# The first layer's value bias and mask move to VectorE and GpSimd, and the second layer's preparation is cut into 28 steps

## What is computed

```python
# layer 0, 16 heads of 16 columns
xn = layer_norm(x, norm_w, norm_b)
q, k = xn @ q_w + q_b, xn @ k_w + k_b
att = softmax(q @ k.T + (1 - mask) * -1e6)          # per head, 256 x 256
v = (xn @ v_w + v_b) * src_mask[:, :, None]
y = att @ v
scale, shift = split(silu(emb) @ emb_w + emb_b)
x = x + silu(layer_norm(y) * (1 + scale) + shift) @ out_w + out_b
# layer 1: linear attention (softmax of q over the head's columns, of k over the rows),
# y = q @ (k.T @ v), then the same scale, shift, silu and product with film_out_W
```

## Time and profile before

| | |
|---|---|
| median of 3 runs | 976.47 us (976.24 to 977.93) |
| the profiled execution's own time | 977.76 us |
| its span | 976.0 us |
| mean granted TensorE clock | 0.982 |
| busy: PE | 916.1 us, 94% |
| busy: DVE | 772.6 us, 79% |
| busy: ACT | 709.6 us, 73% |
| busy: POOL | 581.9 us, 60% |

### The profile page before, as it was taken

One profiled execution on the slowest core, in us unless ns is written; L12 is line 12 of the kernel. 1 busy time (PEld: TensorE's weight loads), 2 busy tenths in 40 slices (PEclk: granted clock), 3 DMA queues, 4 the chain that ended last, 5 costly groups with the idle time before them and its releaser, 6 DMA issues.

```text
span 976.0 us, 24849 instructions
## 1 busy us (share of the span) xinstructions
PE 916.1 (94%) x8880; PEld 760.1 (78%) x8880; DVE 772.6 (79%) x1536; ACT 709.6 (73%) x1328; POOL 581.9 (60%) x1033
## 2 busy tenths in 40 slices
PE   5789999999999999999999767999999999999996
PEld 4666767777777777777776436999999999999995
DVE  5568988888888888888887733888888888888874
ACT  2257677777777777777777665788888888888874
POOL 3343636454545555555554224688888888888874
PEclk9999999999999999999999978999999999999998
DMA  8733333334343434343424112212233222223101
GB/s 263 242 113 116 136 137 136 138 123 150 115 158 118 154 115 159 112 156 115 158 103 147 67 60 86 68 45 77 77 91 99 78 76 77 77 86 97 43 29 54
DMA packets 77402, 108.62 MB, mean 111 GB/s; under 512 B 7072, under 2 KB 43392, under 8 KB 77152
## 3 DMA queue, kind: packets, MB, share of 16 engines
q1 hardware_dynamic: 77280, 107.03, 32.6%
HBM read 35.60 MB, written 16.88 MB: 54 GB/s over the span
## 4 chain that ended last, share of the span: by engine, by line
PE 82%; DVE 8%; issue 6%; POOL 2%; ACT 1%; SPq 0%; DMA 0%; POOLq 0%; DVEq 0%; ACTq 0%
PE psX L1041 14%; PE psY L1141 13%; PE psM L1041 10%; PE psT L1041 9%; PE psM L1120 8%; PE psT L1105 7%; PE psY L1041 4%; PE psT L1289 3%; PE psT L1052 3%; PE psM L1052 3%; PE psY L1258 3%; DVE sb_cm L808 3%; PE psY L1160 2%; DVE sb_yr L825 2%; PE psX L1052 1%
## 5 line engine op out<-in xcount | busy, mean ns | idle before, releaser
L808 DVE TENSOR_REDUCE sb_cm<-psM 128x4 f32<-128x1024 f32 x256 | 313.3, 1224 | 86.6 <-PE psM L1120 77.8
L516 ACT ACTIVATE sb_P<-psT 128x1024 f32<-128x1024 f32 x256 | 262.1, 1025 | 16.9 <-PE psT L1105 13.6
L1141 PE MATMUL psY<-sb_P,sb_Vp 128*17 128x256 f32 x2048 | 137.9, 387 | 8.9 <-DVE sb_yr L825 8.3
L372 POOL TENSOR_SCALAR sb_ve<-sb_mv 128x2 f32<-128x2 f32 x32 | 7.1, 221 | 230.8 <-DVE sb_mv L833 230.8
L1120 PE MATMUL psM<-sb_Ks,sb_Qs 64*128 64x256 f32 x1024 | 118.5, 309 | 11.8 <-DVE sb_cm L808 11.6
L1105 PEld LDWEIGHTS psT<-sb_Qs,sb_Ks 64*128 64x128 f32 x1024 | 78.2, 188 | 60.2 <-issue 53.8
L1105 PE MATMUL psT<-sb_Qs,sb_Ks 64*128 64x256 f32 x1024 | 120.0, 313 | 0.0
L530 ACT ACTIVATE sb_qp<-psX,sb_bq 128x256 f32<-128x256 f32 x122 | 51.2, 471 | 74.8 <-PE psX L1041 74.8
L1120 PEld LDWEIGHTS psM<-sb_Ks,sb_Qs 64*128 64x128 f32 x1024 | 77.5, 186 | 32.9 <-DVE sb_cm L808 17.3
L1041 PE MATMUL psX<-sb_xT,sb_W0h 128*128 128x256 f32 x488 | 95.3, 298 | 1.9 <-DVE sb_xT L815 1.1
L1141 PEld LDWEIGHTS psY<-sb_P,sb_Vp 128*17 128x17 f32 x2048 | 49.4, 97 | 53.3 <-issue 15.6
(11 more groups left out here) (179 smaller groups left out, 2445.2 us busy)
## 6 DMA issues: line engine op xcount, KB each, us to landing
sb_Qs<-sb_qp SPq DMA_DIRECT2D x96, 256.0 KB
sb_Ks<-sb_qp SPq DMA_DIRECT2D x96, 256.0 KB
sb_xt<-in_x SPq DMA_DIRECT2D x32, 256.0 KB, 3.1
y_normed<-sb_Yn SPq DMA_DIRECT2D x32, 256.0 KB, 2.0
sb_u<-in_x SPq DMA_DIRECT2D x32, 256.0 KB, 2.9
sb_u<-y_normed SPq DMA_DIRECT2D x32, 256.0 KB, 3.1
out<-sb_w SPq DMA_DIRECT2D x32, 256.0 KB, 2.2
sb_v<-key_mask SPq DMA_DIRECT2D x32, 128.0 KB, 3.5
```

What stands on the lines that cost most here:

```text
L516: a.activation(P[G % 4][:, :], psT[G % 2][:, :], ACT.Exp).then_inc(s_ex, 1)
L808: v.tensor_reduce(cm[n % 2][:, 4 * j:4 * j + 4], psMM[:, :].rearrange("p (k t) -> p k t", k=4), AX.X, ALU.max, negate=True).then_inc(s_mx, 1)
L1141: ins = pe.matmul(psY[32 * j:32 * j + 17, 0:T], Vp[n % RING][:, m, 4 * gr + j, :], Pj[:, c0:c0 + 256], start=(m == 0), stop=(m == 1))
```

## The change

The bias matmuls are gone from `vals`, with their tiles `vbx` and `c64`, the two DVE instructions that made `vbx`, and PE's wait for them. In their place DVE has `vbias` in slot 7, behind the `reduce`: one tensor_tensor of 128x512 that adds the bias row (`rb`, in SBUF) to the values in PSUM and writes the new SBUF tile `vb`. It is that instruction which now releases `psX`: PE's next `xturn` waits for `s_vb`. `vmask` goes from ACT to POOL, as two tensor_scalar of 128x256 from `vb` to `Vp`, at the end of slot 7 behind `xnorm`.

The second layer's operands are made in 28 steps (`for_later`), three in each round from round 5 on, at the end of slots 2, 4 and 6 of DVE, so ahead of the `reduce` of slots 3, 5 and 7; the last is in round 14. A step is two small film instructions, or one half (128x256) of a weight's high or low part, or one whole `Woh`, or one half of a `Wol`. The semaphores count accordingly.

```diff
-        vbx = sb("vbx", [128, D])
-        c64 = sb("c64", [128, 128])
+        vb = sb("vb", [128, 2, D])
...
-            sp.wait_ge(p_pool, 3)
+            sp.wait_ge(p_pool, 2)
...
-            g.memset(c64[:, :], 1.0 / 64).then_inc(p_pool, 1)
...
+            def vmask(n):
+                if n == 0:
+                    g.wait_ge(p_act, 1)
+                g.wait_ge(s_vb, n + 1)
+                if n >= RING:
+                    g.wait_ge(s_pv, 4 * (n - RING) + 4)
+                for k in range(2):
+                    ins = g.tensor_scalar(Vp[n % RING][:, k, :, 0:16], vb[:, k, :].rearrange("p (h d) -> p h d", d=DH),
+                                          mT[:, k, n:n + 1], 1.0, ALU.mult, ALU.mult)
...
                     if i == 7 and t >= 1 and ok(t + 1):
                         xnorm(t + 1)
+                    if i == 7 and ok(t):
+                        vmask(t)
...
-            def vmask(n):
-                a.wait_ge(s_vm, n + 1)
-                if n >= RING:
-                    a.wait_ge(s_pv, 4 * (n - RING) + 4)
-                for k in range(2):
-                    ins = a.activation(Vp[n % RING][:, k, :, 0:16],
-                                       home("v", n)[:, 256 * k:256 * k + 256].rearrange("p (h d) -> p h d", d=DH),
-                                       ACT.Identity, scale=mT[:, k, n:n + 1])
-                ins.then_inc(s_v, 1)
...
+            def film(m):
+                if m < 2:
+                    v.wait_ge(p_act, 7)
+                    for d in range(2):
+                        v.tensor_scalar(sc[:, m, d, :], ev[:, m, d, :], col[:, m, 8 + d:9 + d], 1.0, ALU.add, ALU.add)\
+                            .then_inc(p_film, 1)
+                elif m < 6:
+                    l, d = divmod(m - 2, 2)
+                    v.wait_ge(p_film, 6)
+                    v.tensor_scalar(FA[:, l, d, :], sc[:, l, d, :], col[:, l, 12 + d:13 + d], 0.5, ALU.mult, ALU.mult)\
+                        .then_inc(p_film, 1)
+                    v.scalar_tensor_tensor(FB[:, l, d, :], sc[:, l, d, :], col[:, l, 14 + d:15 + d], ev[:, l, 2 + d, :],
+                                           ALU.mult, ALU.add).then_inc(p_film, 1)
+                elif m < 8:
+                    v.wait_ge(p_film, 14)
+                    for d in range(2):
+                        v.tensor_scalar(FB[:, m - 6, d, :], FB[:, m - 6, d, :], col[:, m - 6, 10 + d:11 + d], 0.5, ALU.add,
+                                        ALU.mult).then_inc(p_film, 1)
+                else:
+                    v.wait_ge(s_ld[3], 16 * LOADS[3])
+                    for k in range(2 * m - 16, 2 * m - 14):
+                        v.tensor_copy(BD[:, k, 128:136], diag[:, 0:128].rearrange("p (h e) -> p h e", e=DH)[:, :, 0])\
+                            .then_inc(p_film, 1)
+            def second_weight(n, part, k):
                 if part == 0:
+                    v.tensor_scalar(W1h[:, n, k, :].bitcast(F32R), W[1][n][:, k, :], col[:, 1, k:k + 1], None, ALU.mult)\
+                        .then_inc(s_w1, 1)
                 else:
+                    v.wait_ge(s_w1, 4 * n + 2)
+                    v.scalar_tensor_tensor(W1l[:, n, k, :].bitcast(F32R), W[1][n][:, k, :], col[:, 1, k:k + 1],
+                                           W1h[:, n, k, :], ALU.mult, ALU.subtract).then_inc(s_w1, 1)
+            def out_weight(l, m):
+                if m == 0:
                     v.tensor_copy(Woh[l][:, :, :].bitcast(F32R), Wo[l][:, :, :]).then_inc(s_wo, 1)
                 else:
+                    v.wait_ge(s_wo, 3 * l + 1)
+                    v.tensor_tensor(Wol[l][:, m - 1, :].bitcast(F32R), Wo[l][:, m - 1, :], Woh[l][:, m - 1, :],
+                                    ALU.subtract).then_inc(s_wo, 1)
+            def for_later(m):
+                if m < 10:
+                    film(m)
+                elif m < 22:
+                    second_weight((m - 10) // 4, (m - 10) // 2 % 2, m % 2)
+                elif m < 28:
+                    out_weight((m - 22) // 3, (m - 22) % 3)
...
+            def vbias(n):
+
+                v.wait_ge(s_vm, n + 1)
+                if n == 0:
+                    v.wait_ge(p_vb, 1)
+                else:
+                    v.wait_ge(s_v, n)
+                v.tensor_tensor(vb[:, :, :], home("v", n).rearrange("p (k d) -> p k d", k=2),
+                                rb[:, 0:1, :].to_broadcast([128, 2, D]), ALU.add).then_inc(s_vb, 1)
 
...
-                    v.wait_ge(p_vb, 1)
-                    v.tensor_copy(vbx[:, :].bitcast(F32R), rb[:, 0, :]).then_inc(p_vb, 1)
-                    v.wait_ge(p_vb, 2)
-                    v.tensor_tensor(vbx[64:128, :].bitcast(F32R), rb[64:128, 0, :], vbx[64:128, :], ALU.subtract)\
-                        .then_inc(p_vb, 1)
...
-                if t == 5 and i % 2 == 1:
-                    film(i // 2)
-                if t in (6, 7, 8) and i in (1, 5):
-                    scaled(1, t - 6, i // 4)
-                if t in (9, 10) and i in (1, 5):
-                    out_weight(t - 9, i // 4)
...
+                if i == 7 and ok(t):
+                    vbias(t)
...
+                if i in (2, 4, 6) and t >= 5:
+                    for_later(3 * (t - 5) + i // 2 - 1)
...
-                    pe.wait_ge(s_v, n)
+                    pe.wait_ge(s_vb, n)
...
-                    product(dst, (xT, xT2), (W0h[:, 2, :, :], W0l[:, 2, :, :]), o=k, last=False)
-                    if n == 0 and k == 0:
-                        pe.wait_ge(p_vb, 3)
-                    ins = pe.matmul(dst, c64[:, :].bitcast(F32R), vbx[:, :].bitcast(F32R), start=False, stop=True)
+                    ins = product(dst, (xT, xT2), (W0h[:, 2, :, :], W0l[:, 2, :, :]), o=k)
...
-                    pe.wait_ge(s_wo, 4)
+                    pe.wait_ge(s_wo, 6)
...
-                    pe.wait_ge(s_w1, 6)
+                    pe.wait_ge(s_w1, 12)
```

More of the change, by code:

```diff
@@ L179, in bass_cond_seq_kernel @@
         s_in = [[sem(f"s_{c}in{i}") for i in range(RING)] for c in "qk"]
-        s_vm, s_v = sem("s_vm"), sem("s_v")
+        s_vm, s_vb, s_v = sem("s_vm"), sem("s_vb"), sem("s_v")
         s_sm, s_mx, s_cx, s_ct, s_cs = (sem(f"s_{n}") for n in ("sm", "mx", "cx", "ct", "cs"))
@@ L400, in csplit @@
                 g.tensor_tensor(lo.bitcast(F32R), c, hi, ALU.subtract).then_inc(s_cx, 1)
-            g.wait_ge(p_pool, 3)
+            def vmask(n):
[7 more added lines that the diff above has]
+                                          mT[:, k, n:n + 1], 1.0, ALU.mult, ALU.mult)
+                ins.then_inc(s_v, 1)
+            g.wait_ge(p_pool, 2)
             xnorm(0)
@@ L406, in _ @@
             ins.then_inc(p_pool, 1)
-            g.wait_ge(p_pool, 4)
+            g.wait_ge(p_pool, 3)
             def xb_(n):
@@ L707, in slot @@
                     cturned(t - 2)
-                if i == 7 and ok(t):
-                    vmask(t)
                 exps(t, i)
@@ L746, in _ @@
             v.tensor_tensor(mp[:, 1, :].bitcast(F32R), mr2[:, :], mp[:, 0, :], ALU.subtract).then_inc(p_ve, 1)
[L748 to L760, removed]
@@ L762, in first_weight @@
             def first_weight(n):
                 v.wait_ge(s_lw[n], 16)
-                scaled(0, n, 0)
-                scaled(0, n, 1)
-            def out_weight(l, part):
-                if part == 0:
+                for k in range(2):
+                    ins = v.tensor_scalar(W0h[:, n, k, :].bitcast(F32R), W[0][n][:, k, :], col[:, 0, k:k + 1], None,
+                                          ALU.mult)
+                ins.then_inc(s_w0, 1)
+                v.wait_ge(s_w0, 2 * n + 1)
+                for k in range(2):
+                    ins = v.scalar_tensor_tensor(W0l[:, n, k, :].bitcast(F32R), W[0][n][:, k, :], col[:, 0, k:k + 1],
+                                                 W0h[:, n, k, :], ALU.mult, ALU.subtract)
@@ new lines, in first_weight @@
+                ins.then_inc(s_w0, 1)
+            v.wait_ge(s_ld[1], 16 * LOADS[1])
+            first_weight(0)
+            def film(m):
[21 more added lines that the diff above has]
+                            .then_inc(p_film, 1)
@@ L1034, in _, with product @@
         def _(pe):
-            def product(dst, lhs, rhs, o=None, r=None, last=True):
+            def product(dst, lhs, rhs, o=None, r=None):
                 def part(a, d, k):
@@ L1040, in product @@
                 for m, (a, b, d) in enumerate(terms):
-                    ins = pe.matmul(dst, part(lhs[a], d, o), part(rhs[b], d, r), start=(m == 0), stop=(last and m == 5))
+                    ins = pe.matmul(dst, part(lhs[a], d, o), part(rhs[b], d, r), start=(m == 0), stop=(m == 5))
                 return ins
@@ L1294, in tr_ @@
                 if n == 0:
-                    pe.wait_ge(s_v, B)
+                    pe.wait_ge(s_vb, B)
                 pe.wait_ge(e_xn, n + 1)
@@ L1349, in slot @@
                     pe.wait_ge(s_w0, i)
-                if (t, i) == (0, 6):
-                    pe.wait_ge(p_pool, 2)
```

(4 more changed lines are left out.)

31 lines of the change are left out of this document (1 added, 30 removed).

## The result

The changed kernel takes 962.74 us (median of 4 executions, 960.39 to 965.31) against 976.36 us before. The ratio is 0.9863, with a 95% interval from 0.9836 to 0.9891: by the ratio 13.4 us less, give or take 2.7; the two medians lie 13.6 us apart. Direction and mechanism were right, the gain was forecast 11.1 us, some 2.6 us too small.

A forecast was written before the change was run, and what follows sets the result against it. PE, 82% of the chain, sets the pace up to slot 0's `reduce`, then DVE to slot 1. Bias 6.6 + steps 3.7 + start 0.8 = 11.1 us less: median from 976.47 to 965.4 us, range 963.0 to 971.0.

The forecast's parts named there:

- The bias matmuls: Two on PE between slots 6 and 7, 0.12 us each; removing them gains 6.6 us net, from 3.1 to 7.8.
- the give-back: PE's `xturn` waits for `vbias`, about 0.1 us late; mostly absorbed, it returns 0.02 us a round, 0.5 in all.
- The part for rounds 1 and 2: Without `values` yet, DVE and PE wait for each other more tightly in slots 7 and 0: 0.3 us taken off.
- `vbias` at nothing, if covered: On DVE behind slot 7's `reduce`: 0.69 us within 0.67 us of idle time, margin 0.06; uncovered, 21 us.
- The rival in which DVE takes PE's place: Slot 0's `reduce` is late and DVE's stretch eats the 0.24 us a round: 972.0 us if all lost; chance 0.12.
- The slower rival: `vbias` held up by POOL's `xnorm` or by `vmask`, taking 1.25 us each round: 980.1 us; chance 0.06.
- half of the 6.6 us lost: Milder case of DVE taking PE's place, with half of the bias gain lost: forecast at 968.4 us.
- `vmask` on POOL: Mask moved from ACT in slot 7: costs nothing on POOL, 1.10 us there; possible gain 0.0 to 0.1 a round.
- The steps: 28 preparation steps in DVE's idle time, rounds 5 to 14: remove 4.39 us of delay, gain 3.7, from 2.2 to 4.4.
- the eight long steps: Weight-half steps ahead of slots 3 and 7, 0.0 to 0.3 us too long, 0.09 each: 0.7 us lost.
- a rival: Steps gain little: most of the eight long ones blocked by POOL, 3.2 us lost for 0.7: 967.9 us; chance 0.09.
- The start: Round 0: PE's 0.35 us wait for `vbx` and two bias weight loads go, gaining 0.8 us, from 0 to 1.3.

The follow-up runs named there:

- `vbias` twice: The changed kernel with `vbias` done twice in slot 7, the second waiting for the first and releasing `psX`: 989.53 us, one execution.
- the start-alone kernel: The kernel before, with batch 0 alone having its bias from DVE and mask from POOL, and `vbx` made later: 973.58 us, ratio 0.9974.

## Why the prediction was right or wrong

*The bias matmuls: right.* 0.12 us each was forecast and 0.24 a round found with nothing in their place. The forecast of 6.6 us is what the traces give (6.6). The mechanism is right in its parts: `reduce` of slot 0 isn't later, `xturn` is late by 0.15 where I had 0.1, and the give-back is 0.026 us a round for 0.02. The part for rounds 1 and 2 (0.3 us) can't be told from chance.

*`vbias` at nothing, if covered: right,* and `vbias` twice shows what it costs without cover. The rival in which DVE takes PE's place fails by the same row: all but 0.026 of the 0.24 stays. The slower rival fails by the durations of L835, 680 to 682 ns; in the steady round POOL's `xnorm` is drawn to its end 0.05 us before `vbias` begins and the mask begins after it, so it is the order of the slot that keeps them apart. Three slips of the prediction change nothing: with half of the 6.6 us lost the time would be 968.7 and not 968.4; the `reduce` that starts 0.05 behind the drawn end of its matmuls in rows 3 is slot 7's and not slot 0's; and the range's upper end is 971.2 by the sum and 971.0 where the chances are given.

*`vmask` on POOL: right.* That the old place on ACT cost nothing holds only while the bias was PE's: behind `vbias` and the exponential it costs 0.72 us a round.

*The steps: the sum right, 3.9 us for 3.7, its working wrong.* I had the eight long steps in slots 2 and 6 overrun and those of slot 4 fit. It is the other way round: slots 2 and 6 show 0.32 to 0.45 us, and slot 4 0.74 to 1.01. Nor did I price the two whole `Woh` (steps 22 and 25), which stand in slot 4 and make rounds 12 and 13 longer by 0.14 and 0.08, half of what the steps cost. The trace of before had said so in film's 545 ns, and the Trainium skill (SBUF — State Buffer, "Who interferes with whom") names the forms: two SBUF inputs or a two-port mode, blocked by a GpSimd instruction that came first. The traces of the changed kernel agree (0.45 against 1.01 us). I weighed the rule, priced it at 0.8 us and left it to a rival, because the longest low half in the old slot 5 had taken but 0.73 us. These rows of the trace of before (timelines of POOL and DVE) suggest why that was cheap:

```profile
116.12 1.29 POOL L389 TENSOR_TENSOR sb_qp<-sb_qp 128x512 fp32r<-128x512 f32 x1
...
116.97 1.11 DVE L758 SCALAR_TENSOR_TENSOR sb_W1l<-sb_W,sb_col,sb_W1h 128x256 fp32r<-128x256 f32 x2
```

The pair began 0.85 us into the subtract and lost 0.23 us in all (1.11 against 0.88), shared between two instructions. In its new place the single one begins 0.56 us into it (157.04 against 156.48) and loses 0.56.

*The start: too small, and the step that failed.* It was forecast at 0.8 us. It is 1.5 (0.8 to 2.1) by the start-alone kernel at equal clock, 2.5 (1.1 to 4.0) by its totals, and 0.9 to 1.5 by the traces, 0.9 where the low halves are blocked. So its size is known to half a microsecond at best, and 0.8 lies at or below the lower edge of each. The term counted PE's drawn wait and two weight loads of one trace, in which the low halves had taken the block and `vbx` none. In other executions `vbx` is blocked instead. I read one outcome of a race as its price. A trace of one execution can't show the other, but this line of the trace of before (durations in ns) should have asked for it, one half at 1477 where the others take 484:

```profile
L758 DVE SCALAR_TENSOR_TENSOR sb_W0l<-sb_W,sb_col,sb_W0h x6: 477/484/1477, 10.3 to 19.3; 128x256 fp32r<-128x256 f32 x6
```

*The total.* 6.6 + 3.9 + 1.5 = 12.0 us, and the fit gives 12.1. That makes 976.47 - 12.1 = 964.4, in the range. The start term is 0.7 us of the miss and the steps 0.2. The measured 962.74 is 1.7 us below 964.4, and that is the larger part. Two things can account for it, neither of them shown: the granted clock was higher in the changed kernel's executions (worth 0.9 us over all of them), and this is a median of four executions that spread over 5 us. My range held the unknown costs only. Its low end, 963.0, is the sum of the tops of three terms (7.8 + 4.4 + 1.3); it put the start at no more than 1.3, and it had nothing for the clock or the scatter of the measurement, though the three runs shown had a spread of 1.7 us. That the direction and the places of the gain came out is the mechanism's doing; how far below 964.4 this one median fell is, as far as the runs show, chance.

## What to carry to other kernels

Work moved to an engine that is nearly full costs only what exceeds the idle time at that exact place: read the idle time ahead of the next instruction, and subtract what the same change takes from it. A step of two SBUF inputs, or a copy or scaling from SBUF to SBUF, that is put beside a long GpSimd instruction on SBUF can double its time; ask for each slot what GpSimd runs there before asking how long DVE is idle. And look in the start of a kernel for a long instruction that overlaps another engine's: its duration may be one side of a race. In the same program the pair of low halves took 0.88 or 2.29 us, and batch 1's `xturn` came at 20.67 or 23.30. Before such a program is compared with another, look at where its granted clock is missing: here it was in the start, between the layers and at the end, outside the steady rounds.

## What the runs showed of the hardware

- A tensor_tensor with one input in PSUM and one in SBUF isn't disturbed by GpSimd: the divide (128x256) takes 423 to 425 ns in 64 cases, those of slot 4 beside GpSimd's 1.3 us subtract (156.70 within 156.48 to 157.77 in the changed kernel's first trace), and batch 0's `vbias` (128x512) took 0.69 us beside that subtract where the others take 0.68. In the steady rounds `vbias` had no GpSimd instruction beside it.
- A blocked instruction is drawn longer, with no idle time ahead of it on its engine: scalar_tensor_tensor of 128x256 took 0.45 us free and up to 1.01 us beside GpSimd's 1.3 us subtract; a cast of 128x512 0.42 and 1.01.
- The mean granted clock of an execution goes from 0.980 to 0.991 in the same program on one chip, and the time goes with it by 0.485 us for each 0.001. Between two traces at 0.982 and 0.991, some 4 us of the difference go with the clock. In all 14 traces the granted clock is 1.00 from 80 to 520 us and from 620 to 940; the lower level (0.50 in some stretches) appears in the start, between the layers and at the end.
